# The expert stage of a gated cross-attention block: spreading routing weights over the rows by DMA instead of by a TensorE product, on one Trainium2 core

## The chip, the core and the metric

The kernel runs on one core of one Trainium2 chip. The metric is the device time of one execution in microseconds (us), lower is better. A core has five engines that run side by side, each in its own program order, and that wait for each other through semaphores: PE (TensorE, matrix products into PSUM), DVE (VectorE), ACT (ScalarE), POOL (GpSimd) and SP (SyncE, which here only issues DMAs). SBUF is the working memory of 128 partitions (rows), PSUM the memory that PE writes, in eight banks of 128x512 floats, DRAM the memory of the chip. "PE" in a row of the profile is the matmul itself, "PEld" the load of its stationary operand.

## The reference, cut to what matters

x has 32 batches of 128 tokens with 128 features. The block has four steps, each added to x with a gate: cross attention (stage a), a mixture of eight experts (stage b), a second cross attention with 16 heads (stage c), a second mixture (stage d). The change touches stage b and its two boundaries. Stage b computes:

```python
logits = jnp.einsum('bsd,de->bse', input, Wg)          # input = layernorm(x), E = 8 experts
probs = jax.nn.softmax(logits, axis=-1)
top_vals, top_idx = jax.lax.top_k(probs, TOP_K)        # TOP_K = 2
top_vals = top_vals / jnp.sum(top_vals, axis=-1, keepdims=True)
onehot = jax.nn.one_hot(top_idx, E, dtype=input.dtype)
mask = jnp.sum(onehot, axis=2)
scores = jnp.sum(onehot * top_vals[..., None], axis=2)
xm = input[None] * jnp.moveaxis(mask, -1, 0)[..., None]
h = jnp.einsum('ebsd,edh->ebsh', xm, W1) + b1[:, None, None, :]     # H = 256
h = jax.nn.relu(h)
y = jnp.einsum('ebsh,ehd->ebsd', h, W2) + b2[:, None, None, :]
out = jnp.sum(y * jnp.moveaxis(scores, -1, 0)[..., None], axis=0)
x = x + jnp.tanh(g_ffn[0]) * out
```

All is float32. Products are made from operands that are split in a high and a low part (hi, lo), three PE products each (hi by hi, hi by lo, lo by hi).

## The kernel before

The 32 batches are worked in 8 groups (NG) of 4 batches, 512 tokens (GT) each. In stage b the tokens lie along the columns and the features along the 128 rows. `pipeline` writes each engine's program: `step(a, m, t)` is called with the group m whose experts run, the group a after it, for which things are made ready, and the group t before it, which is finished. Two steps stand in a loop (Fori), the first two and the last are written out. "Group 0" to "group 7" below are the values of m.

Every expert e of a group goes through these steps, all 128 rows high and with two chunks (HC) of 512 columns:

- up (`up`, `hidden_of`): six PE products from xh, xl and W1 into two PSUM banks (L371 to L373); two sets of banks, taken in turn
- relu (L930): ACT adds the bias and writes b_hr, one ACTIVATE for each chunk
- spread (L861): one PE product of a 0/1 matrix with st, which lays row e of the routing weights over all 128 rows, into a PSUM bank; this is the "PE product" of the change
- scale (L978): DVE multiplies b_hr by the spread weights and writes b_hs
- high (L805): ACT rounds b_hs to b_hh; low (L811): DVE writes b_hl = b_hs - b_hh
- down (`down`): six PE products with W2 that add into the bank Y, three experts (LAG) behind up

b_hr, b_hs, b_hh and b_hl have two halves, expert e uses half e % 2. PE runs up e, spread e, down e-3; ACT runs relu e, high e-1; DVE runs scale e, low e-1. Around these, once per group: the weights of the next group are placed in ss (`dve_place`, after expert 0 on DVE), turned by four PE transposes (`place`, expert 2) and copied to st by ACT (`act_place`, expert 3). The finished Y of the group before is copied by ACT ahead of relu 3 (L815), turned back by PE in expert 4 (`y_back`), which also waits for st because both use the bank MISC, added to x by DVE (`dve_residual`) with the statistics of the next layer norm, POOL makes 1/std, DVE norms in expert 5, and xh and xl of the next stage are made in expert 7.

At the front boundary, in the last step of stage a, DVE does the routing of groups 0 to 6 in one piece (`route.first`, `route.second`, then, after xl, `route.weights`); group 7's (`tail`) is done in the first group of stage b, in three pieces at experts 1, 3 and 5. Between them stands the late setup: constants of stage c on DVE (`dve_setup_late`, expert 4), two PE products (L436, L437, expert 5) and an ACT copy (expert 6). At the back boundary, in the last group of stage b and behind it, the first three units of stage c are prepared (`c_prepare`): keys, queries and values of its first group. SP then writes the split keys and queries to DRAM and reads them back spread over partitions, before the first scores (L1177, L1178).

The lines of the profile that the text speaks of, inside the functions that are printed below:

## Time and profile before

| what | us |
|---|---|
| median of 3 runs (their range) | 766.39 (763.78 to 766.4) |
| the profiled execution | 767.7 |
| its span in the trace | 765.9 |
| busy: PE, DVE, ACT, POOL | 649.0, 560.2, 426.0, 104.2 |
| mean granted clock of PE | 0.908 of full speed |
| stage b, from its first relu to the last value of Y (141.85 to 365.9) | 224 |

The profile is of one execution. Busy times of engines overlap, so they don't add up to the span. A row of the timeline is one instruction, or several alike that follow each other (x2 and so on); "[4.67 <-DVE exp_scale L427]" behind it says how long its engine had stood idle and which instruction ended that. A granted clock of 1.00 is 2.4 GHz, of 0.50 is 1.2 GHz.

### The profile page before, as it was taken

How to read it: one execution, taken by the hardware profiler on the slowest of the kernel's cores; microseconds unless marked ns; L12 is line 12 of the kernel's file. 1: busy time of each engine (PE TensorE's matmuls, PEld its weight loads, DVE VectorE, ACT ScalarE, POOL GpSimd, SP SyncE). 2: the span in 40 equal slices, each digit the busy share in tenths (PEclk: the TensorE clock that was granted, in tenths of full speed). 3: DMA queues.
4: the chain of work that ended last, by engine and by line, in shares of the span. 5: the costliest groups of instructions: out<-in, count | busy, mean ns of one | idle time of the engine just before them, and what ended most of it. 6: DMA issues, size and time to landing. Idle time of an engine off the chain costs nothing.

```text
span 765.9 us, 12807 instructions
## 1 busy us (share of the span) xinstructions
PE 649.0 (85%) x4078; PEld 503.5 (66%) x4078; DVE 560.2 (73%) x1281; ACT 426.0 (56%) x665; POOL 104.2 (14%) x133
## 2 busy tenths in 40 slices
PE   5865654979999999979599988988988489999996
PEld 3644443657787787757377666766756267888884
DVE  3567565687898898868478668668676669888885
ACT  3333321467777777756277666656766145555553
POOL 3444230020000000000401022022022100000000
PEclk8677665889999999999799999999999679999998
DMA  5312000000000000010244124224210000000000
GB/s 159 101 63 98 29 8 0 1 0 1 1 0 0 0 0 0 0 43 28 50 121 121 54 67 119 69 49 119 69 42 2 0 1 0 15 14 14 27 14 28
DMA packets 23698, 29.24 MB, mean 38 GB/s; under 512 B 3313, under 2 KB 17522, under 8 KB 23666
## 3 DMA queue, kind: packets, MB, share of 16 engines
q1 hardware_dynamic: 23666, 28.84, 13.1%
...
## 4 chain that ended last, share of the span: by engine, by line
PE 63%; DVE 18%; issue 6%; POOL 5%; ACT 5%; DMA 1%; DVEq 1%; SPq 0%; POOLq 0%; ACTq 0%
PE psum L371 12%; PE psum L373 11%; PE psum L372 11%; PE psum L1187 6%; PE psum L1202 3%; PE psum L1177 2%; DVE stats L281 2%; POOL rstd L293 2%; PE psum L360 2%; PE psum L1178 2%; DVE b_hl L811 2%; DVE xn L300 2%; DVE c_mx L1356 2%; PE psum L1503 2%; PE psum L319 1%
## 5 line engine op out<-in xcount | busy, mean ns | idle before, releaser
L371 PE MATMUL psum<-xh,w_hi 128*128 (+1 forms) x248 | 104.1, 420 | 5.2 <-DVE w_lo L1346 3.0
L1297 ACT ACTIVATE c_pt<-psum 77x512 f32<-77x512 f32 x128 | 74.5, 585 | 49.9 <-PE psum L1187 49.8
L372 PE MATMUL psum<-xl,w_hi 128*128 (+1 forms) x248 | 100.3, 404 | 0.0
L373 PE MATMUL psum<-xh,w_lo 128*128 (+1 forms) x248 | 100.1, 404 | 0.0
L930 ACT ACTIVATE b_hr<-psum,b1s 128x512 f32<-128x512 f32 x128 | 80.8, 686 | 24.0 <-PE psum L373 23.9
L978 DVE TENSOR_TENSOR b_hs<-b_hr,psum 128x1024 f32<-128x1024 f32 x64 | 77.9, 1217 | 21.7 <-ACT b_hr L930 20.4
L811 DVE TENSOR_TENSOR b_hl<-b_hs,b_hh 128x1024 fp32r<-128x1024 f32 x64 | 78.3, 1223 | 16.9 <-ACT b_hh L805 16.9
L805 ACT ACTIVATE b_hh<-b_hs 128x1024 fp32r<-128x1024 f32 x64 | 67.9, 1061 | 34.1 <-PE psum L373 32.2
L1187 PE MATMUL psum<-ident,c_pf 128*77 128x128 f32 x512 | 75.9, 286 | 0.0
L1187 PEld LDWEIGHTS psum<-ident,c_pf 128*77 128x77 f32 x512 | 59.4, 152 | 14.9 <-issue 10.4
L1302 ACT ACTIVATE c_pf<-c_sm,zero_col,exp_scale 128x616 f32<-128x616 f32 x64 | 57.3, 895 | 17.8 <-DVE c_sm L1362 17.8
L1356 DVE TENSOR_REDUCE c_mx<-psum 128x8 f32<-128x616 f32 x64 | 51.0, 797 | 19.8 <-PE psum L1178 19.2
L371 PEld LDWEIGHTS psum<-xh,w_hi 128*128 128x128 f32 x248 | 48.2, 195 | 17.5 <-DVE w_lo L1346 3.4
L1362 DVE TENSOR_TENSOR c_sm<-psum,c_mx 128x616 f32<-128x616 f32 x64 | 51.2, 800 | 6.5
L373 PEld LDWEIGHTS psum<-xh,w_lo 128*128 128x128 f32 x248 | 47.9, 193 | 11.7
L372 PEld LDWEIGHTS psum<-xl,w_hi 128*128 128x128 f32 x248 | 48.2, 194 | 9.5
L805 ACT ACTIVATE d_hh<-d_hs 128x512 fp32r<-128x512 f32 x56 | 35.4, 632 | 31.3 <-DVE d_hs L1598 17.5
L371 PE MATMUL psum<-b_hh,w_hi 128*128 128x512 f32 x128 | 51.5, 403 | 1.4 <-DVE b_hl L811 1.3
L1553 ACT ACTIVATE d_hr<-psum 128x512 f32<-128x512 f32 x56 | 33.4, 597 | 32.7 <-PE psum L373 31.6
...
L1177 PE MATMUL psum<-mask_bf,ident_bf 128*128 128x312 bf16 x128 | 39.1, 312 | 13.9 <-DVE c_sm L1362 10.8
L373 PE MATMUL psum<-b_hh,w_lo 128*128 128x512 f32 x128 | 50.8, 397 | 0.0
...
## 6 DMA issues: line engine op xcount, KB each, us to landing
w_hi<-c_q_spread SPq DMA_DIRECT2D x24, 256.0 KB
...
ctxg<-in_ctxT SPq DMA_DIRECT2D x16, 156.0 KB, 4.1
...
x_all<-in_x SPq DMA_DIRECT2D x8, 256.0 KB, 2.7
out_dram<-x_all SPq DMA_DIRECT2D x8, 256.0 KB, 2.3
...
```

What stands on the lines that cost most here:

```text
L371: pe.matmul(o, wh, h, start=start, stop=False)
L372: pe.matmul(o, wh, l, start=False, stop=False)
L373: return pe.matmul(o, wl, h, start=False, stop=stop)
L805: a_.activation(*self.high(q), ACT.Copy).then_inc(self.hi_done, 1)
L811: v.tensor_tensor(o, i0, i1, ALU.subtract).then_inc(self.lo_done, 1)
L930: ins = a_.activation(Bb["hr"][:, q, c, :], Z[q][c], ACT.Relu, bias=b1s[:, e, c:c + 1])
L978: v.tensor_tensor(Bb["hs"][:, q, :, :], Bb["hr"][:, q, :, :], SBC[q].unsqueeze(1).broadcast_to([P, HC, GT]), ALU.mult).then_inc(xb.scaled, 1)
L1177: pe.matmul(o, ident_bf[:], mask_bf[:].unsqueeze(1).broadcast_to([P, HQ, SK]), start=True, stop=False)
L1187: ins = pe.transpose(bank[2 + q % 2][0:S2, j * P:(j + 1) * P], pf1[:, h % 2, (q % 2) * HQ + j, :], ident[:])
L1297: a_.activation(pt[:, q % NC4, :], bank[2 + q % 2][0:S2, :], ACT.Copy).then_inc(pt_done, 1)
L1302: a_.activation(pf1[:, h % 2, :, :], sm1[:, h % 2, :, :], ACT.Exp, bias=zero_col[:, 0:1], scale=exp_scale[:, 0:1]).then_inc(s1_exp, 1)
L1356: v.tensor_reduce(mm, s, AX.X, ALU.max).then_inc(s1_max, 1)
```

## The change

From group 1 on, row e of the weights comes to the 128 rows by DMA. ss gets a third block, hi + lo (`dve_place`), which the same transposes turn; ACT copies its 8 rows to lt_s; SP stores them to DRAM in two DMAs (b_rows) and reads each row back to all 128 partitions, into one of four slots (SLOTS) of the new tile b_bc. DVE scales with that tile. Group 0 keeps the PE product. To make room, b_hr and b_hs are now the same buffer, and relu waits for `lo_done` where it waited for `scaled`. The routing's second half and the late setup move ahead of stage b (its PE products to bank 5, between the router's product and its transposes); the tail's routing is cut in eight pieces; the prepared units of stage c move from experts 0, 1 (PE) and 1, 2 (ACT, DVE) to 0, 2 and 1, 3; in the last group y_back, residual and norm come one expert later; behind the last group ACT copies xh before it copies the values; SP loads the first context of stage c ahead of its new work.

```diff
@@ pe_setup_late, act_setup_late: bank[7] -> bank[5]
@@ pe_a step
                     lg0.pe_product(pe, t)
+                    if not m:
+                        pe_setup_late(pe)
                     lg0.pe_transpose(pe, t)
@@ act_a step
                     lg0.act_copy(a_, t)
                     if not m:
+                        act_setup_late(a_)
                         Route(0, HEAD, rt_tail).act_ratio(a_)
@@ dve_a step
                         route.first(v)
-                        route.second(v)
...
                     ln1.dve_low(v, t)
                     if not m:
+                        route.second(v)
+                        dve_setup_late(v)
                         route.weights(v)
@@ buffers of stage b
-        B = dict(hr=sb("b_hr", [P, 2, HC, GT]), hs=sb("b_hs", [P, 2, HC, GT]),
+        SLOTS = 4
+        b_hr = sb("b_hr", [P, 2, HC, GT])
+        B = dict(hr=b_hr, hs=b_hr,
                  hh=sb("b_hh", [P, 2, HC, GT], F32R), hl=sb("b_hl", [P, 2, HC, GT], F32R),
-                 y=sb("b_y", [P, 2, GT]))
+                 y=sb("b_y", [P, 2, GT]), bc=sb("b_bc", [P, SLOTS, GT]))
@@ dve_place
-                v.tensor_copy(ss[:, p, :, 32:32 + E], sc_l[:, a.tiles(), :].bitcast(F32)).then_inc(self.ss_ready, 1)
+                v.tensor_copy(ss[:, p, :, 32:32 + E], sc_l[:, a.tiles(), :].bitcast(F32))
+                v.tensor_tensor(ss[:, p, :, 64:64 + E], sc_h[:, a.tiles(), :].bitcast(F32),
+                                sc_l[:, a.tiles(), :].bitcast(F32), ALU.add).then_inc(self.ss_ready, 1)
@@ act_place
+                if self is xb and not self.first(a):
+                    a_.activation(lt_s[64:64 + E, a.parity, :], misc[64:64 + E], ACT.Copy).then_inc(self.rows_done, 1)
                 a_.activation(st[:, a.parity, :], misc, ACT.Copy).then_inc(self.st_done, 1)
@@ new: SP in stage b, ahead of its work for stage c
+        def sp_b(sp):
+            c_prepare["sp"](sp)
+            def step(a, m, t):
+                if not a or xb.first(a):
+                    return
+                p = a.parity
+                sp.wait_ge(xb.rows_done, a.at(1, 0))
+                sp.dma_start(xb.rows_dram[p, 0:4, :], lt_s[64:68, p, :]).then_inc(xb.rows_out[p], 16)
+                xb.before(sp, xb.scaled, a, 0, SLOTS)
+                sp.dma_start(xb.rows_dram[p, 4:E, :], lt_s[68:64 + E, p, :]).then_inc(xb.rows_out[p], 16)
+                for e in range(E):
+                    if e == 0:
+                        sp.wait_ge(xb.rows_out[p], a.pair(32, 32 * p))
+                    else:
+                        xb.before(sp, xb.scaled, a, e, SLOTS)
+                    sp.dma_start(Bb["bc"][:, e % SLOTS, :],
+                                 xb.rows_dram[p, e:e + 1, :].broadcast_to([P, GT])).then_inc(xb.spread_in[e % SLOTS], 16)
@@ pe_b: up, step
-                xb.before(pe, xb.scaled, g, e, 2)
-                pe.matmul(SBC[q], sel0[:, e, :], st[:, g.parity, :], start=True, stop=True).then_inc(xb.bc_ready, 1)
+                if xb.first(g):
+                    xb.before(pe, xb.scaled, g, e, 2)
+                    pe.matmul(SBC[q], sel0[:, e, :], st[:, g.parity, :], start=True, stop=True).then_inc(xb.bc_ready, 1)
...
-                    if m and e == 4 and t:
+                    if m and e == (4 if a else 5) and t:
                         y_back(a, m, t)
...
-                    if m and not a and e < 2:
-                        c_prepare["pe"](pe, e)
+                    if m and not a and e in (0, 2):
+                        c_prepare["pe"](pe, e // 2)
...
-                    if m and e == 5 and xb.first(m):
-                        pe.wait_ge(xb.st_done, 2)
-                        pe_setup_late(pe)
@@ act_b: relu, step
                 xb.before(a_, xb.z_ready, g, e, 0)
-                xb.before(a_, xb.scaled, g, e, 2)
+                xb.before(a_, xb.lo_done, g, e, 2)
...
-                        if xb.first(m) and e == 3:
+                        if xb.first(m) and e == 6:
                             tail.act_ratio(a_)
...
-                        c_prepare["act"](a_, 2)
                         ln2.act_high(a_, t)
+                        c_prepare["act"](a_, 2)
@@ dve_b: scale, step
-                xb.before(v, xb.bc_ready, g, e, 0)
-                xb.before(v, xb.lo_done, g, e, 2)
+                if xb.first(g):
+                    xb.before(v, xb.bc_ready, g, e, 0)
+                    spread = SBC[q]
+                else:
+                    v.wait_ge(xb.spread_in[e % SLOTS], g.at(32, 16 * (e // SLOTS + 1) - 32))
+                    spread = Bb["bc"][:, e % SLOTS, :]
                 v.tensor_tensor(Bb["hs"][:, q, :, :], Bb["hr"][:, q, :, :],
-                                SBC[q].unsqueeze(1).broadcast_to([P, HC, GT]), ALU.mult).then_inc(xb.scaled, 1)
+                                spread.unsqueeze(1).broadcast_to([P, HC, GT]), ALU.mult).then_inc(xb.scaled, 1)
```

Three places in the order of instructions, each in the loop over the middle groups. On ACT, one expert and the start of the next, before:

```order
L930 ACTIVATE b_hr<-psum,b1s 128x512 [waits b_hidden_scaled,b_hidden_ready]
L930 ACTIVATE b_hr<-psum,b1s 128x512
L805 ACTIVATE b_hh<-b_hs 128x1024 [waits b_hidden_used,b_hidden_scaled]
L778 REGISTER_ALU
L930 ACTIVATE b_hr<-psum,b1s 128x512 [waits b_hidden_scaled,b_hidden_ready]
```

and now:

```order
L985 ACTIVATE b_hr<-psum,b1s 128x512 [waits b_hidden_low,b_hidden_ready]
L985 ACTIVATE b_hr<-psum,b1s 128x512
L838 ACTIVATE b_hh<-b_hr 128x1024 [waits b_hidden_used,b_hidden_scaled]
L807 REGISTER_ALU
L985 ACTIVATE b_hr<-psum,b1s 128x512 [waits b_hidden_low,b_hidden_ready]
```

The order is the same; the relu waits for b_hidden_low (counted by low on DVE) in place of b_hidden_scaled (counted by scale). On PE, up of an expert and down of the one three behind it, before:

```order
L371 MATMUL psum<-xh,w_hi 128x512 [waits b_hidden_read]
L372 MATMUL psum<-xl,w_hi 128x512
L373 MATMUL psum<-xh,w_lo 128x512
L371 MATMUL psum<-xh,w_hi 128x512
L372 MATMUL psum<-xl,w_hi 128x512
L373 MATMUL psum<-xh,w_lo 128x512
L861 MATMUL psum<-st,w_hi 128x512 [waits b_hidden_scaled]
L371 MATMUL psum<-b_hh,w_hi 128x512 [waits b_hidden_low]
L372 MATMUL psum<-b_hl,w_hi 128x512
```

and now:

```order
L371 MATMUL psum<-xh,w_hi 128x512 [waits b_hidden_read]
L372 MATMUL psum<-xl,w_hi 128x512
L373 MATMUL psum<-xh,w_lo 128x512
L371 MATMUL psum<-xh,w_hi 128x512
L372 MATMUL psum<-xl,w_hi 128x512
L373 MATMUL psum<-xh,w_lo 128x512
L371 MATMUL psum<-b_hh,w_hi 128x512 [waits b_hidden_low]
L372 MATMUL psum<-b_hl,w_hi 128x512
L373 MATMUL psum<-b_hh,w_lo 128x512
```

The spread product between up and down is gone. On DVE, scale and low of two experts, before:

```order
L978 TENSOR_TENSOR b_hs<-b_hr,psum 128x1024 [waits b_hidden_low,b_spread_ready,b_hidden_read]
L811 TENSOR_TENSOR b_hl<-b_hs,b_hh 128x1024 [waits b_hidden_high,b_hidden_used]
L778 REGISTER_ALU
L978 TENSOR_TENSOR b_hs<-b_hr,psum 128x1024 [waits b_hidden_low,b_spread_ready,b_hidden_read]
L811 TENSOR_TENSOR b_hl<-b_hs,b_hh 128x1024 [waits b_hidden_high,b_hidden_used]
```

and now:

```order
L1049 TENSOR_TENSOR b_hr<-b_hr,b_bc 128x1024 [waits b_spread_loaded2,b_hidden_read]
L844 TENSOR_TENSOR b_hl<-b_hr,b_hh 128x1024 [waits b_hidden_high,b_hidden_used]
L807 REGISTER_ALU
L1049 TENSOR_TENSOR b_hr<-b_hr,b_bc 128x1024 [waits b_spread_loaded3,b_hidden_read]
L844 TENSOR_TENSOR b_hl<-b_hr,b_hh 128x1024 [waits b_hidden_high,b_hidden_used]
```

The order is again the same; scale works in place on b_hr, takes the factor from b_bc and waits for its DMA.

## Rows read from the trace of the kernel before

**Rows 1.** The page, part 4: the chain that ended last, by engine.
```profile
PE 63%; DVE 18%; issue 6%; POOL 5%; ACT 5%; DMA 1%; DVEq 1%; SPq 0%; POOLq 0%; ACTq 0%
```

**Rows 2.** Windows of groups 0, 2, 7: stretch, length, busy by engine, clock, DMA.
```profile
core 0: us, PE busy (x) PEld busy (x) DVE busy (x) ACT busy (x) POOL busy (x), PEclk, DMA share, GB/s
141.85:170.24 28.39, 23.13 (x92) 17.98 (x93) 24.07 (x44) 17.69 (x28) 4.26 (x1) 0.88 0.00 1
...
196.41:222.66 26.25, 26.18 (x119) 21.02 (x118) 22.51 (x35) 19.95 (x27) 1.42 (x3) 1.00 0.00 1
327.70:366.00 38.30, 32.63 (x131) 24.30 (x129) 26.72 (x36) 21.53 (x30) 1.26 (x2) 0.96 0.10 35
```

**Rows 3.** Timeline of PE, group 1: start, duration, engine, line, operation, tiles.
```profile
172.99 0.40 PE L861 MATMUL psum<-st,w_hi 128*128 128x512 f32 x1
...
176.01 0.40 PE L861 MATMUL psum<-st,w_hi 128*128 128x512 f32 x1
```

**Rows 4.** Timeline of ACT, groups 0 and 7.
```profile
154.81 1.26 ACT L930 ACTIVATE b_hr<-psum,b1s 128x512 f32<-128x512 f32 x2
155.95 1.06 ACT L805 ACTIVATE b_hh<-b_hs 128x1024 fp32r<-128x1024 f32 x1
...
339.67 1.26 ACT L930 ACTIVATE b_hr<-psum,b1s 128x512 f32<-128x512 f32 x2 [4.47 <-PE psum L373]
342.26 1.06 ACT L805 ACTIVATE b_hh<-b_hs 128x1024 fp32r<-128x1024 f32 x1 [1.33 <-DVE b_hs L978]
```

**Rows 5.** Timeline of DVE, groups 1 and 7.
```profile
187.87 0.69 DVE L826 TENSOR_TENSOR x_all<-psum,x_all 128x512 f32 x1
...
189.79 1.19 DVE L978 TENSOR_TENSOR b_hs<-b_hr,psum 128x1024 f32<-128x1024 f32 x1
190.90 1.22 DVE L811 TENSOR_TENSOR b_hl<-b_hs,b_hh 128x1024 fp32r<-128x1024 f32 x1
192.03 1.11 DVE L300 TENSOR_SCALAR xn<-x_all,mv,rstd 128x128 f32 x4
...
340.96 1.22 DVE L978 TENSOR_TENSOR b_hs<-b_hr,psum 128x1024 f32<-128x1024 f32 x1 [4.39 <-ACT b_hr L930]
343.42 1.23 DVE L811 TENSOR_TENSOR b_hl<-b_hs,b_hh 128x1024 fp32r<-128x1024 f32 x1 [1.24 <-ACT b_hh L805]
```

**Rows 6.** The page, part 5: busy us, mean ns, idle before, releaser.
```profile
L978 DVE TENSOR_TENSOR b_hs<-b_hr,psum 128x1024 f32<-128x1024 f32 x64 | 77.9, 1217 | 21.7 <-ACT b_hr L930 20.4
L811 DVE TENSOR_TENSOR b_hl<-b_hs,b_hh 128x1024 fp32r<-128x1024 f32 x64 | 78.3, 1223 | 16.9 <-ACT b_hh L805 16.9
```

**Rows 7.** Timeline of PE: the two longest holes of stage b.
```profile
159.68 0.77 PE L436 MATMUL psum<-wo,bv 128*128 128x128 f32 x2 [4.67 <-DVE exp_scale L427]
...
161.09 0.80 PE L371 MATMUL psum<-xh,w_hi 128*128 128x512 f32 x1
...
336.62 0.50 PE L371 MATMUL psum<-xh,w_hi 128*128 128x512 f32 x1 [2.99 <-DVE w_lo L1346]
```

**Rows 8.** Windows behind both holes, and one of stage c.
```profile
159.70:163.80 4.10, 4.10 (x10) 3.09 (x11) 4.10 (x3) 0.00 (x0) 3.03 (x1) 0.50 0.00 0
...
336.60:338.10 1.50, 1.48 (x6) 1.24 (x7) 0.00 (x0) 0.00 (x0) 0.00 (x0) 1.00 0.44 173
338.10:341.30 3.20, 3.20 (x9) 2.47 (x8) 0.34 (x1) 1.26 (x2) 0.00 (x0) 0.50 0.24 72
...
475.00:480.00 5.00, 3.86 (x32) 2.81 (x33) 3.38 (x9) 2.40 (x4) 2.92 (x3) 0.80 0.11 22
```

**Rows 9.** Timeline of DVE at the front boundary: end of second, then xl.
```profile
132.12 0.68 DVE L332 TENSOR_TENSOR xl<-psum,xh 128x512 fp32r<-128x512 f32 x1
```

**Rows 10.** Timeline of ACT and PE at the back boundary.
```profile
374.18 0.68 ACT L1291 ACTIVATE c_v<-psum 77x256 f32<-77x256 f32 x2 [7.64 <-POOL c_v L1440]
...
376.10 0.44 PE L1177 MATMUL psum<-mask_bf,ident_bf 128*128 128x312 bf16 x1 [3.14 <-DVE xl L332]
```

**Rows 11.** DMA issues: tiles, queue, count, KB each, us to landing.
```profile
ctxg<-in_ctxT SPq DMA_DIRECT2D x16, 156.0 KB, 4.1
...
x_all<-in_x SPq DMA_DIRECT2D x8, 256.0 KB, 2.7
```

104 lines of the change are left out of this document (71 added, 33 removed).

## The prediction

> **What bounds the kernel now.** I read the page first: PE holds 63% of the chain that ended last, DVE 18% [rows 1]. Then the windows of the expert stage, cut at the first relu of a group: one of the six groups in the middle takes 26.25 us and PE is busy in 26.18 of them, DVE in 22.51, ACT in 19.95, at a granted clock of 1.00; the first group takes 28.39, the last 38.30 [rows 2]. So in the middle PE is the bound and every matmul removed there would pay its whole pitch, if nothing else comes up. The PE timeline gives that pitch: from one spread product (L861) to the next are 3.02 us and 13 matmuls [rows 3], so 0.23 each. ACT and DVE have what an expert needs of them: relu (two ACTIVATEs), scale (L978), high (L805), low (L811) [rows 4, 5]. Both idle a little per expert, waiting for PE [rows 6].
>
> **Part 1: the spread products.** 56 of the 64 L861 go (groups 1 to 7 have 8 each): 8 x 0.23 = 1.84 us of PE per group. PE then needs 26.25 - 1.84 = 24.4 per group. The scale reads its factor from a 128x512 tile in SBUF, not PSUM. Low has both operands in SBUF and takes 1223 ns where scale with one in PSUM takes 1217 [rows 6], so I take no change for it, and bounds of -0.03 to +0.03 per instruction. The Trainium skill ("VectorE: DVE Perf Modes", the section on the TRN2 errata) has a table with 62 cycles less for an SBUF source than for a PSUM source; by that the scale would be an estimated 0.065 us shorter and this sum some 3.6 us lower. The row of low does not bear that out, and the row decides.
>
> **Part 2: relu now waits for low.** b_hr and b_hs become one buffer, scaled in place. Before, ACT's relu of expert e waited for scale e-2; now for low e-2, since high and low of e-2 still read that half. This is the step that matters. The orders are fixed: ACT runs relu e, high e-1, relu e+1; DVE runs scale e, low e-1, scale e+1. So relu e+1 waits for low e-1, low e-1 stands behind scale e on DVE, and scale e waits for relu e. That is a closed loop, and its length is the time per expert. Its pieces from the traces: relu to scale start 340.96 - 339.67 = 1.29 [rows 4, 5]; scale to low, back to back, 190.90 - 189.79 = 1.11, and low to the next 192.03 - 190.90 = 1.13, I take 1.13; low itself 1.22; from the end of a DVE instruction to the ACT that waited for it 342.26 - (340.96 + 1.22) = 0.08, and I take 0.07 as other rows are a little shorter. Sum 1.29 + 1.13 + 1.22 + 0.07 = 3.71 us. High is beside it: it starts 1.14 after relu and ends at 1.14 + 1.06 = 2.20, and low may start 0.10 later (343.42 after 342.26 + 1.06), at 2.30, before scale lets it at 2.42. So 3.71 against 3.02 now: PE, with 12 x 0.23 = 2.8, waits 0.9 us for each expert. Eight experts: 29.7.
>
> **Part 3: what else sits in the loop.** DVE idles from the pitch of low (1.13) to the next scale (1.22 + 0.07 + 1.29 = 2.58): room for 1.45. Residual and statistics at e = 4 take 189.79 - 187.87 = 1.92 [rows 5], 0.45 too much. Norm, the new third write to ss and the xl of the layer norm fit. On ACT the idle time after high is 1.5: the copy of y, st and the new copy of 8 rows to lt_s, each of 512 columns and so some 0.6 by half a relu (1.27 / 2), fit, the last two together with 0.3 to spare. At e = 4 PE's transposes of y wait for st, which now comes behind that copy, and down 1 behind them reaches high 3 about 0.25 late. Sum 29.7 + 0.45 + 0.25 = 30.4. There is also a hole: PE finds nothing from the end of up 3 until y is copied, by the same addition 3.3 us. The trace has one of 2.99 us in the last group [rows 7]: 1.5 us after it the granted clock fell from 1.00 to 0.50 for 3.2 us [rows 8]. The part of it that isn't absorbed by PE's new slack I put at 0.3 (bounds 0 and 1.6, the second if the clock is low at once, as after the 4.67 us hole [rows 7, 8]). Group: **30.7 us** against 26.25, +4.45, six times: **+26.7**.
>
> **Part 4: first and last group.** In the first, the late setup and the tail's routing held PE up 4.67 us at L436 [rows 7]. The setup goes ahead of the stage and the routing is cut into pieces of under 1.45 us that the loop hides. But the loop holds here too: 8 x 3.71 less 3.71 - 1.14 for the two relus that run back to back = 27.1, against 28.39: **-1.2**, though a hole of 4.67 is gone. The last group has 38.30, with the 2.99 us hole at PE (unit 1 of stage c) and 3.2 at half clock. Afterwards: 7 x 3.71 = 26.0, the 0.7 of part 3, and from the last relu 2.42 + 1.13 + 1.22 and 6 matmuls with their end, 1.6 = 6.4; with 0.3 for the clock 33.4: **-4.9**. The later places of the stage c units are in the idle time of ACT and DVE.
>
> **Part 5: the two boundaries.** Ahead of the stage, second now runs after the xl that waited behind it until 132.12 [rows 9], which frees the router product some 2.6 us earlier; but the late setup now stands ahead of act_ratio and of PE's logit transposes: seven short DVE instructions, an estimated 1.1 in all, two PE products, 161.09 - 159.68 = 1.4 at half clock [rows 7], and an ACT copy, 0.4. Against 2.6 that leaves **+0.3** (bounds -2.6 and +3: all of one side, none of the other). Behind the stage ACT does the xh copy before the value copies, which waited 7.64 for POOL's memset; the scores need those value copies too (374.18 + 0.68 = 374.86), and started at 376.10 [rows 10]: **-1.2**, not more. The key and query DMAs come from an SP queue that now issues them behind the last spread; they still have four experts' time.
>
> **Part 6: the DMAs.** SP gets, per group, two stores of 4x512 and eight spreads of 256 KB, four slots deep. A 256 KB load lands in 2.7 us, a 156 KB one in 4.1 [rows 11]. A slot is asked for when scale e-4 ends, so it has three experts, 11 us. Hidden: 0. The bound above is 4.1 each, one after the other, the rival below. First in a group come the second store, its landing and spread 0, about 2 x 2.7 = 5.4 us of some 11. Hidden too.
>
> **Sum.** 26.7 - 1.2 - 4.9 + 0.3 - 1.2 = **+19.7 us**. Against the profiled span of 765.9 that is 785.6. The profiled execution took 767.7, 1.8 more than its span and 0.2% above the median of the runs, 766.39; so the sum can be laid on the median as it is: **786.1**.
>
> **Rivals.** (a) The clock falls to half at once at each group's restart, or more often: high 2 then waits for a down at half rate, 1.6 us a group, so 32.0: 6 x 5.75 - 1.2 - 3.6 - 0.9 = +28.8, 795.2. For it: a stretch of stage c with gaps of about 1 us and PE busy 3.86 of 5 had 0.80 [rows 8]; against: PE's 25% slack absorbs most. The Trainium skill ("TensorE: Matmul & The Clock Gate", the section on a second HAM failure mode) tells of the same swing where PE idles briefly between groups of matmuls. 0.20. (b) The other side: the loop stays under PE's time, and PE keeps the bound. Then groups take 24.4: 6 x -1.85, the first loses its 4.67 hole, the last 4.9 + 1.85, boundaries -0.9: 11.1 + 4.7 + 6.8 + 0.9 = 23.5 less, 742.9. It decides where the loop is under 24.4 / 8 = 3.05 us; low or scale would have to be half as long, and 64 instances of each say 1.22. 0.05. (c) The spreads come one by one at 4.1 us, 32.8 a group: 39.3 - 1.2 - 2.8 - 0.9 = +34.4, 800.8. Against: 2.7 for a load of this size. 0.04. (d) The in-place wait costs less than read and the stage comes out even, within 0.5%: 0.03.
>
> **Numbers.** Forecast 0.68. A measurement of this kernel can tell about 0.5%, 4 us. Faster by more 0.05, within 0.03, slower 0.92. The range takes in the loop with 0.03 for each handover and no clock loss (30.0 a group, -4.2, and -2.6 of the boundary) and rival (a) with its boundary at +3: 779 to 798.
>
> **What would show it.** Right: group period near 30.7; ACT's b_hr waiting for DVE b_hl, over 0.8 us per expert, as the largest wait of ACT; PE's share of the chain falling and DVE's rising; scale at 1.22. Wrong: b_hr waiting for PE (rival b), scale waiting for a DMA (c), half clock over long stretches (a), or scale much under 1.2.

## The result: 5.6% slower, about twice what was predicted

| | kernel before | changed kernel |
|---|---|---|
| median of the runs (range) | 765.21 (763.5 to 767.48) | 808.03 us (804.57 to 813.07) |
| ratio to before, 95% interval | | 1.056 (1.0523 to 1.0598) |
| span of the profiled execution | 765.9 | 805.6 |
| first relu of stage b | 141.85 | 141.23 |
| group 0 | 28.39 | 28.61 |
| groups 1 to 6, mean | 26.24 | 33.33 |
| group 7, to the copy of Y | 38.27 | 37.39 |
| Y to the end of the span | 399.96 | 398.38 |

A group runs from its first relu to that of the next, read from the timeline of ACT. The prediction was 786.1 us, range 779 to 798: the sign is right, the time lies 22 us above it and outside the range. The excess of 39.7 us in the span lies in groups 1 to 6 alone: 6 x (33.33 - 26.24) = 42.5, where the prediction had 26.7. The rest of the program came out 2.8 us shorter.

The page of the changed kernel, part 4 (answers to [rows 1]) and three groups of part 5 (busy us, mean ns, idle before, releaser; answer to [rows 6]):

```profile
PE 45%; DVE 24%; issue 10%; ACT 10%; POOL 8%; DVEq 1%; DMA 0%; ACTq 0%; SPq 0%; POOLq 0%
...
L985 ACT ACTIVATE b_hr<-psum,b1s 128x512 f32<-128x512 f32 x128 | 80.9, 684 | 87.9 <-DVE b_hl L844 81.0
...
L1049 DVE TENSOR_TENSOR b_hr<-b_hr,b_bc 128x1024 f32<-128x1024 f32 x56 | 68.3, 1220 | 52.3 <-ACT b_hr L985 52.3
...
L844 DVE TENSOR_TENSOR b_hl<-b_hr,b_hh 128x1024 fp32r<-128x1024 f32 x64 | 78.0, 1219 | 12.3 <-ACT b_hh L838 12.3
```

PE's share of the chain fell from 63 to 45%. The relu (L985) idles 81.0 us behind low (L844), scale (L1049) 52.3 us behind relu, and never behind a DMA. One turn of the loop, from the timelines of ACT and DVE in group 2:

```profile
207.31 1.27 ACT L985 ACTIVATE b_hr<-psum,b1s 128x512 f32<-128x512 f32 x2 [1.63 <-DVE b_hl L844]
208.61 1.23 DVE L1049 TENSOR_TENSOR b_hr<-b_hr,b_bc 128x1024 f32<-128x1024 f32 x1 [1.12 <-ACT b_hr L985]
209.75 1.22 DVE L844 TENSOR_TENSOR b_hl<-b_hr,b_hh 128x1024 fp32r<-128x1024 f32 x1
211.06 1.26 ACT L985 ACTIVATE b_hr<-psum,b1s 128x512 f32<-128x512 f32 x2 [1.54 <-DVE b_hl L844]
```

1.30 + 1.14 + 1.22 + 0.09 = 3.75 us, as summed (3.71). The windows, cut as in [rows 2], give group 2 and the last:

```profile
203.47:237.08 33.61, 27.39 (x110) 20.12 (x110) 22.63 (x36) 20.08 (x28) 3.29 (x3) 0.95 0.20 63
...
369.83:407.22 37.39, 31.87 (x117) 23.90 (x117) 25.18 (x34) 21.00 (x29) 2.97 (x2) 0.86 0.22 71
```

Group 2 from relu to relu: 3.84 + 3.75 + 3.75 + 5.27 + 4.50 + 4.17 + 4.63 + 3.70 = 33.61. Eight plain experts would be 30.0, so 3.6 us lie in four intervals. **Experts 3 to 5**, timelines of PE and ACT:

```profile
213.81 0.75 PE L927 MATMUL psum<-st,w_hi 128*128 128x512 f32 x1 [3.04 <-ACT b_y L848]
214.36 0.63 PE L928 MATMUL psum<-st,w_lo 128*128 128x512 f32 x1
...
217.59 1.06 ACT L838 ACTIVATE b_hh<-b_hr 128x1024 fp32r<-128x1024 f32 x1 [1.52 <-PE psum L373]
...
222.10 1.06 ACT L838 ACTIVATE b_hh<-b_hr 128x1024 fp32r<-128x1024 f32 x1 [0.75 <-PE psum L373]
```

PE stands 3.04 us for the copy of y (predicted: 3.3). Then its matmuls of 512 columns take 0.63 instead of 0.39, at half the clock, 1.2 of 2.4 GHz (granted 0.51 in the window 213.80 to 217.00, below). High 2 waits 1.52 for down 0. High 3 waits 0.75 for down 1, which stands behind the transposes of y, and these wait 1.04 for st. **Experts 5 and 6**, timelines of DVE and POOL:

```profile
226.33 1.20 DVE L1049 TENSOR_TENSOR b_hr<-b_hr,b_bc 128x1024 f32<-128x1024 f32 x1
226.49 1.08 POOL L257 TENSOR_TENSOR spare_q<-half_neg 1x1 f32<-1x1 f32 x1 [30.29 <-DVE mv L284]
227.44 1.22 DVE L844 TENSOR_TENSOR b_hl<-b_hr,b_hh 128x1024 fp32r<-128x1024 f32 x1
227.55 1.20 POOL L292 TENSOR_SCALAR vpe<-mv 128x4 f32<-128x4 f32 x1
228.83 1.04 POOL L293 TENSOR_TENSOR rstd<-vpe,half_neg 128x4 f32<-128x4 f32 x1
229.90 1.12 DVE L300 TENSOR_SCALAR xn<-x_all,mv,rstd 128x128 f32 x4 [1.24 <-POOL rstd L293]
```

POOL's first operation for 1/std ends as scale does (227.57 and 227.53), its second as low does (228.75 and 228.66). Before, they took 0.18 and 0.22:

```profile
189.96 0.18 POOL L257 TENSOR_TENSOR spare_q<-half_neg 1x1 f32<-1x1 f32 x1 [24.93 <-DVE mv L284]
190.12 0.22 POOL L292 TENSOR_SCALAR vpe<-mv 128x4 f32<-128x4 f32 x1
190.42 1.04 POOL L293 TENSOR_TENSOR rstd<-vpe,half_neg 128x4 f32<-128x4 f32 x1
```

### The profile page after: what moved, and what is told of

Its sections match the earlier page's. It is cut to its first block, busy times and chain, and to the rows that moved or that the text cites. A ratio compares the mean times of both kernels' runs of the same rounds, so it can differ in the third digit from the quotient of the medians.

```text
span 805.6 us, 12850 instructions
## 1 busy us (share of the span) xinstructions
PE 654.0 (81%) x4022; PEld 495.9 (62%) x4022; DVE 558.5 (69%) x1297; ACT 427.4 (53%) x672; POOL 117.3 (15%) x133
## 4 chain that ended last, share of the span: by engine, by line
PE 45%; DVE 24%; issue 10%; ACT 10%; POOL 8%; DVEq 1%; DMA 0%; ACTq 0%; SPq 0%; POOLq 0%
PE psum L371 7%; PE psum L373 7%; PE psum L372 7%; PE psum L1261 5%; DVE b_hl L844 5%; ACT b_hr L985 3%; POOL rstd L293 3%; DVE b_hr L1049 3%; PE psum L1276 3%; DVE xn L300 3%; DVE stats L281 3%; PE psum L1251 2%; ACT b_hh L838 2%; PE psum L360 2%; PE psum L1252 2%
## 5 line engine op out<-in xcount | busy, mean ns | idle before, releaser
L985 ACT ACTIVATE b_hr<-psum,b1s 128x512 f32<-128x512 f32 x128 | 80.9, 684 | 87.9 <-DVE b_hl L844 81.0
L1049 DVE TENSOR_TENSOR b_hr<-b_hr,b_bc 128x1024 f32<-128x1024 f32 x56 | 68.3, 1220 | 52.3 <-ACT b_hr L985 52.3
L844 DVE TENSOR_TENSOR b_hl<-b_hr,b_hh 128x1024 fp32r<-128x1024 f32 x64 | 78.0, 1219 | 12.3 <-ACT b_hh L838 12.3
L838 ACT ACTIVATE b_hh<-b_hr 128x1024 fp32r<-128x1024 f32 x64 | 67.7, 1058 | 14.1 <-PE psum L373 11.3
L371 PE MATMUL psum<-b_hh,w_hi 128*128 128x512 f32 x128 | 57.4, 448 | 12.7 <-DVE b_hl L844 12.7
L257 POOL TENSOR_TENSOR spare_q<-half_neg 1x1 f32<-1x1 f32 x24 | 9.8, 410 | 369.9 <-DVE mv L284 369.9
L319 PE MATMUL psum<-ident,xn 128*128 128x128 f32 x128 | 26.1, 338 | 40.4 <-DVE xn L300 27.7
L372 PE MATMUL psum<-b_hl,w_hi 128*128 128x512 f32 x128 | 53.8, 420 | 0.0
L373 PE MATMUL psum<-b_hh,w_lo 128*128 128x512 f32 x128 | 53.4, 418 | 0.0
```

What stands on the lines that cost most here:

```text
L371: pe.matmul(o, wh, h, start=start, stop=False)
L372: pe.matmul(o, wh, l, start=False, stop=False)
L373: return pe.matmul(o, wl, h, start=False, stop=stop)
L838: a_.activation(*self.high(q), ACT.Copy).then_inc(self.hi_done, 1)
L844: v.tensor_tensor(o, i0, i1, ALU.subtract).then_inc(self.lo_done, 1)
L985: ins = a_.activation(Bb["hr"][:, q, c, :], Z[q][c], ACT.Relu, bias=b1s[:, e, c:c + 1])
```

## The experiments

Each was timed beside the kernel before, and its ratio is to those runs, whose medians were 766.4 to 767.2 us. "1 to 6" is the mean of groups 1 to 6, "tail" the stretch from the last relu of stage b to the copy of Y, all read from the timeline of ACT.

| kernel | median us | ratio (95% interval) | group 0 | 1 to 6 | last | tail |
|---|---|---|---|---|---|---|
| before (profiled) | 765.21 | 1 | 28.39 | 26.24 | 38.27 | 8.43 |
| changed | 808.03 | 1.056 (1.0523, 1.0598) | 28.61 | 33.33 | 37.39 | 9.92 |
| e4_in_place_alone | 806.41 | 1.0514 (1.0481, 1.0547) | 33.11 | 31.50 | 40.18 | 7.15 |
| e5_placement_alone | 758.61 | 0.9878 (0.9834, 0.9923) | 20.84 | 26.24 | 33.91 | 9.54 |
| e1_two_buffers | 763.14 | 0.9955 (0.9931, 0.9979) | 20.83 | 26.97 | 36.28 | 12.43 |
| e2_early_y | 809.58 | 1.0554 (1.0514, 1.0593) | 28.64 | 33.49 | 37.97 | 9.90 |
| e3_psum_factor | 799.34 | 1.0427 (1.0395, 1.046) | 28.64 | 31.76 | 36.11 | 8.68 |
| e9_expert5_psum | 801.64 | 1.0465 (1.0414, 1.0516) | 28.62 | 31.78 | 37.36 | 9.90 |
| e8_no_hole | 806.73 | 1.0511 (1.0463, 1.0559) | 29.27 | 32.74 | 38.11 | 9.93 |
| e11_hole_and_pool | 796.55 | 1.0407 (1.034, 1.0474) | 28.30 | 31.35 | 36.61 | 9.92 |
| e14_last_transposes | 809.97 | 1.0594 (1.0549, 1.0639) | 28.63 | 33.04 | 41.11 | 13.61 |
| e15_last_expert6 | 809.17 | 1.0543 (1.0495, 1.0591) | 28.61 | 33.24 | 35.60 | 8.90 |
| e17_last_norm | 806.89 | 1.0544 (1.0508, 1.0581) | 28.62 | 33.03 | 38.66 | 8.36 |
| e10_all | 764.21 | 0.9971 (0.9943, 0.9999) | 22.23 | 26.68 | 34.87 | 10.81 |
| e13_best | 759.34 | 0.9902 (0.987, 0.9933) | 20.84 | 25.78 | 39.98 | 16.09 |
| **e16_two_buffers_psum5_6** | **752.19** | 0.9801 (0.9775, 0.9828) | 20.83 | 25.77 | 35.20 | 11.05 |
| e18_two_buffers_norm | 751.19 | 0.9823 (0.9782, 0.9863) | 20.83 | 25.78 | 34.58 | 8.67 |

### The wait for low: the loop

e4_in_place_alone, on the kernel before (b_pad keeps the addresses of the rest; the last two lines are relu's wait; "..." in a diff stands for lines left out):

```diff
-        B = dict(hr=sb("b_hr", [P, 2, HC, GT]), hs=sb("b_hs", [P, 2, HC, GT]),
+        b_hr, pad = sb("b_hr", [P, 2, HC, GT]), sb("b_pad", [P, 2, HC, GT])
+        B = dict(hr=b_hr, hs=b_hr,
...
-                xb.before(a_, xb.scaled, g, e, 2)
+                xb.before(a_, xb.lo_done, g, e, 2)
```

> The kernel before with one part of the change alone: b_hr scaled in place and relu waiting for low e-2. Spread products on PE, no DMAs, boundary work where it was. Theory of the loop: 3.75 us per expert, 31 to 33 us a group against 26.25, and the holes of the first and last group come on top: 800 to 812 us. Rival, that the DMA path is what costs: 764 to 772.

e1_two_buffers, on the changed kernel (to make room, the spread has 2 slots and b_y one half; a transfer of 16 bytes carries one wait on SP; the last lines are relu's wait and scale's):

```diff
-        B = dict(hr=b_hr, hs=b_hr,
+        B = dict(hr=b_hr, hs=sb("b_hs", [P, 2, HC, GT]),
...
-                xb.before(a_, xb.lo_done, g, e, 2)
+                xb.before(a_, xb.scaled, g, e, 2)
...
+                xb.before(v, xb.lo_done, g, e, 2)
```

> The changed kernel with b_hr and b_hs apart again: relu waits for scale e-2, scale for low e-2, as before the change. To make the room, the spread tile has two slots in place of four and b_y one half; the two stores of the rows go out together. Theory of the loop (relu, scale, low e-1, relu): the loop is cut, PE's 24.4 us or the spreads set the group, 24.4 to 26.3 us a group, 750 to 768 us in all. Rival, that the DMA spreads or the moved boundary work cost the time: groups stay over 30 us and the time over 790.

With the wait alone, the kernel before goes to 806.41; without it, the changed kernel to 763.14. A stretch of eight experts of each, from the windows; that of e4 runs from relu 3 of group 2 to relu 3 of group 3, that of e1 is its group 2:

```profile
218.53:248.98 30.45, 27.00 (x119) 20.78 (x119) 22.38 (x34) 19.33 (x27) 1.42 (x3) 1.00 0.00 0
```

```profile
192.80:219.76 26.96, 25.22 (x111) 19.30 (x111) 22.51 (x36) 20.57 (x29) 3.29 (x3) 1.00 0.28 80
```

The first, of e4, has no transfer in it and all spread products, and takes 30.45 us, close to the 30.4 of the prediction's sum without its clock term. In part that is luck: the 0.25 for high 3 is not in it (e4 has no copy of 8 rows), and the 0.04 by which a turn is longer than summed, eight times, fills its place. The wait alone costs nearly as much as the whole change, and the transfers are not what costs. It doesn't cost it in the same places: in groups 1 to 6 e4 loses 6 x (31.50 - 26.24) = 31.6 us of the 42.5 of the changed kernel, and 6.6 more in its first and last group, where the work of the boundaries still has its old places. The second, of e1 with two slots, shows it once more: 80 GB/s run beside a group of 26.96.

### The placement alone

e5_placement_alone: the spread products of all groups and both buffers are back, stores and spread transfers are gone, the new places of the boundary work stay. The lines are in PE's spread and in relu's wait.

```diff
-                if xb.first(g):
+                if True:
...
-                xb.before(a_, xb.lo_done, g, e, 2)
+                xb.before(a_, xb.scaled, g, e, 2)
```

> Edit, on the changed kernel: the spread products of TensorE for all groups, relu and scale in separate buffers as before, neither the stores of the eight rows nor the transfers that spread them; what stays is the placement of the boundary work anew (setup ahead of the stage, the tail's routing cut in pieces, the earlier pieces of the next stage, three blocks of ss). Theory (the placement is no part of the slowdown and gives back some of the holes of the first and the last group and of the boundary behind the stage): groups 1 to 6 at 26.2 us as before, 3 to 6 us gained outside them: 760 to 764 us. Rival (the placement costs part of the slowdown, by new holes or by work in other queues): 768 us or more.

It is 1.2% faster than the kernel before, with groups of 26.24 us as there. Its first group takes 20.84, where [rows 2] has 28.39 and a clock of 0.88: the hole of 4.67 us in [rows 7] is gone and with it the half clock.

```profile
145.00:165.84 20.84, 20.26 (x88) 15.99 (x89) 19.06 (x32) 17.69 (x27) 4.28 (x1) 1.00 0.00 0
```

The gain is more than the 3 to 6 us expected. In the changed kernel the loop takes it back: 28.61, and e1, without the loop, has 20.83.

### POOL held up by DVE

e3_psum_factor: in groups 1 to 7, too, scale reads a factor from PSUM, a stale one of group 0; their weighting by their own weights is left out.

```diff
-                    spread = Bb["bc"][:, e % SLOTS, :]
+                    spread = SBC[q]
```

> The changed kernel, but DVE's scale takes its factor from the PSUM bank that group 0 left, in all groups; the DMAs and their waits stay. It leaves out that groups 1 to 7 are scaled with their own weights. Theory that POOL stands still while DVE works on two SBUF operands: POOL's two short instructions ahead of 1/std take 0.2 each again and not 1.1 and 1.2, norm no longer waits, relu 5 to 6 and 6 to 7 go to 3.75 each; 1.3 us less per group and some 2 to 3 at the end of the last, 796 to 800 us. Rival, that POOL is late because of the DMAs or of low: POOL as in the changed kernel, within 2 us of 808.

e9_expert5_psum keeps the spread product for expert 5 alone:

```diff
-                if xb.first(g):
+                if xb.first(g) or e == 5:
...
+                    if e == 5:
+                        v.wait_ge(xb.bc_ready, g.at(1, 8))
+                        spread = SBC[q]
```

> Edit, on the changed kernel: for expert 5 of every group TensorE's spread product stays and the scale of expert 5 takes its second operand from PSUM; the transfer of that row and all other experts stay as they are. It is the scale that ran beside GpSimd's subtraction for the standard deviation. Theory (a VectorE operation with both operands in SBUF holds up GpSimd's two tiny operations for the normalisation, 1.08 and 1.20 us instead of 0.18 and 0.22, and VectorE then waits 1.24 us for their result): the subtraction goes back to about 0.2 us; the second one, beside the product low of expert 5 which has both operands in SBUF in the kernel before too, where it was not held up, also; relu 5 to relu 7 falls from 8.8 us to about 7.5, a group by 1.3, seven groups by 9: time 798 to 801 us. Rival (the late standard deviation comes from somewhere else, or only moves the wait): 806 to 809 us.

Both give POOL its short times back, here e9, DVE and POOL:

```profile
224.75 1.19 DVE L1052 TENSOR_TENSOR b_hr<-b_hr,psum 128x1024 f32<-128x1024 f32 x1
224.92 0.18 POOL L257 TENSOR_TENSOR spare_q<-half_neg 1x1 f32<-1x1 f32 x1 [29.72 <-DVE mv L284]
225.08 0.22 POOL L292 TENSOR_SCALAR vpe<-mv 128x4 f32<-128x4 f32 x1
225.38 1.04 POOL L293 TENSOR_TENSOR rstd<-vpe,half_neg 128x4 f32<-128x4 f32 x1
225.86 1.22 DVE L844 TENSOR_TENSOR b_hl<-b_hr,b_hh 128x1024 fp32r<-128x1024 f32 x1
227.00 1.11 DVE L300 TENSOR_SCALAR xn<-x_all,mv,rstd 128x128 f32 x4
```

POOL starts 0.17 us behind scale here and 0.16 in the changed kernel, so that it is the operand that differs and not the moment. Relu 6 to relu 7 falls from 4.62 to 3.76, 0.87 a group, not the 1.3 expected: relu 5 to relu 6 stays at 4.17, which is residual and statistics. The mean group falls by 1.55; the rest is the clock, which in e9 fell in only three of these six groups. The Trainium skill ("SBUF — State Buffer", the section "SBUF: two separate sides") says that a DVE instruction with two SBUF inputs and a POOL instruction that reads SBUF exclude each other, and that the second waits for the whole of the first; for POOL behind DVE the rows agree, to 0.1 us. For DVE behind POOL they don't: above, low with its two SBUF inputs starts 0.48 us into POOL's 1/std, and neither takes longer.

### The hole and the clock

e2_early_y copies Y one expert earlier:

```diff
-                        if e == LAG and t:
+                        if e == LAG - 1 and t:
                             xb.act_y(a_, t, Y)
```

> The changed kernel with ACT's copy of y ahead of relu 2 in place of relu 3. Theory of the clock: the 3.0 us hole of PE in front of b2 goes, the clock stays at 1.00 behind it, down 0 takes 1.4 and not 2.5, and relu 3 to relu 4 falls from 5.27 to about 3.9; 1.3 to 1.6 us less per group, 797 to 800 us in all against 808. Rival, that the low clock lies in slack and relu 4 is late by something else: within 2 us of 808.

The hole only moved, behind st, and the half clock with it (PE of e2):

```profile
218.70 1.11 PE L853 MATMUL psum<-ident,b_y 128*128 128x128 f32 x4 [4.23 <-ACT st L832]
...
220.04 0.63 PE L372 MATMUL psum<-b_hl,w_hi 128*128 128x512 f32 x1
```

e8_no_hole adds to this the placement one expert earlier on PE and ACT:

```diff
-                    if m and e == 2 and a:
+                    if m and e == 1 and a:
                         place(a)
...
-                        if e == 3 and a:
+                        if e == 2 and a:
                             xb.act_place(a_, a, MISC)
```

> Edit, on the changed kernel: the copy of the Y bank stands before expert 2 on ScalarE instead of before expert 3, the placement before expert 1 on TensorE instead of before expert 2, and ScalarE's copies of its result before expert 2 instead of before expert 3, so that neither the b2 matmul nor the transposes of y find their operand late. In the changed kernel relu 3 to relu 4 took 5.27 us and relu 4 to relu 5 4.50 where a plain expert takes 3.75. Moving the copy of Y alone left the sum of two experts at 9.75 us, with a new hole of 4.23 us at the transposes. Theory (TensorE's holes of 3 to 4 us at the boundary bring the granted clock to half, and the work behind them runs at half): without the hole the two intervals come to about 8.3 us together instead of 9.77, a group to about 31.9 instead of 33.3 us, and seven groups with a boundary give 8 to 10 us: a span of about 796 us, time 797 to 800. Rival (the boundary costs what it does through ScalarE's and VectorE's queues, whatever TensorE's clock): 805 to 809 us, as the changed kernel.

e11_hole_and_pool is e8 and e9 together.

> Edit, on the changed kernel: both edits together, the boundary's copies and the placement moved as in the one and expert 5's factor from PSUM as in the other. Theory (the two are independent, and with both gone a group is what the prediction summed without a clock term: eight times 3.71 plus 0.7 = 30.4 us): group about 30.5 us, seven intervals of groups 20 us shorter than in the changed kernel: time 787 to 791 us. Rival (they share one cause, or each only hides the other): no less than the better of the two alone, 797 us or more.

e8 reached 806.73, not 797 to 800: a hole of some 2.4 us came up at the placement, behind ss. In groups 2 and 3 of e8 (PE, then windows):

```profile
208.31 0.66 PE L825 MATMUL psum<-ident,ss 128*128 128x128 f32 x4 [2.47 <-DVE ss L819]
...
241.76 0.66 PE L825 MATMUL psum<-ident,ss 128*128 128x128 f32 x4 [2.43 <-DVE ss L819]
```

```profile
204.23:237.66 33.43, 27.58 (x110) 20.01 (x110) 22.45 (x36) 19.86 (x28) 3.28 (x3) 0.95 0.21 64
237.66:269.61 31.95, 25.87 (x111) 18.97 (x111) 22.58 (x36) 19.87 (x28) 3.28 (x3) 1.00 0.20 66
```

Two like holes, one with the clock down behind it and one without; the difference, 1.5 us, is what this fall costs. The same in the changed kernel and e9, both with a hole of 3.04 us that ends at 213.81, 213.80 to 217.00 of each:

```profile
213.80:217.00 3.20, 3.19 (x8) 2.51 (x9) 1.81 (x2) 1.26 (x2) 0.00 (x0) 0.51 0.28 87
```

```profile
213.80:217.00 3.20, 3.19 (x14) 2.55 (x14) 1.81 (x2) 2.19 (x3) 0.00 (x0) 1.00 0.30 87
```

8 matmuls in one, 14 in the other. Groups 2 and 5 of e9 are 31.16 and 32.70. So the length of a hole alone doesn't say whether the clock falls. In the changed kernel it fell in all six groups (mean 0.95 in each), and what that cost depends on when: relu 3 to relu 4 took 4.88 to 5.27 us in five of them and 4.15 in group 4, where the half clock came 1.5 us behind the hole and met only the last two of down 0's six products:

```profile
280.72 0.50 PE L927 MATMUL psum<-st,w_hi 128*128 128x512 f32 x1 [3.04 <-ACT b_y L848]
...
281.98 0.47 PE L371 MATMUL psum<-b_hh,w_hi 128*128 128x512 f32 x1
282.24 0.63 PE L372 MATMUL psum<-b_hl,w_hi 128*128 128x512 f32 x1
```

A fall thus cost 0.4 to 1.5 us there, 1.2 in the mean. The Trainium skill ("TensorE: Matmul & The Clock Gate", the section "What's actually happening") calls the gate's activity window free-running. By that, the moment at which a hole comes would count besides its length; that fits these pairs, but no run shows it. e11 gives the sum of both edits: five of its six groups took 31.01 to 31.29 us (clock 1.00 in groups 2 and 3), one 32.64. That is some 0.7 above the 30.4 without clock term: 0.45 more in the interval at the placement (4.20 instead of 3.75), 0.3 in the turn of the loop, 0.2 in two intervals of 3.85, less the 0.25 of high 3, which waits no longer. Its time, 796.55, lies 6 us above the range expected; for six groups these 0.7 and the one fall are 5.7 of them.

### The last group

e14_last_transposes puts PE's transposes of the norm of group 6 behind two down products:

```diff
-                    if m and e == 7 and t:
+                    if a and e == 7 and t:
                         ln2.pe_transpose(pe, t)
+                    if t and not m and e == 1:
+                        ln2.pe_transpose(pe, Group(None, NG - 2))
```

> Edit, on the changed kernel: in the last group only, TensorE's transposes for the normalisation of the group before stand behind the second product of experts 5 and 6 instead of ahead of them. In the changed kernel TensorE waited there 4.55 us for the normalised rows and then ran nine matmuls and more at half the clock, and from relu 7 to the copy of Y it took 9.9 us, where the prediction had 6.4. Theory (the transposes in a queue that runs in order hold up two products whose operands are there, and the hole halves the clock behind them): the hole shrinks to about 1.5 us or less in one piece, relu 7 to the copy of Y takes 7 to 7.6 us: the span shorter by 2.3 to 2.9 us, time about 805 us. Rival (the tail is set by VectorE's chain of norm, scale 7, xl and low 7 alone): 9.5 to 9.9 us, no gain.

e15_last_expert6, in the last group alone:

```diff
-                if xb.first(g):
+                if xb.first(g) or (g.i is None and g.c == NG - 1 and e == 6):
...
+                    if g.i is None and g.c == NG - 1 and e == 6:
+                        v.wait_ge(xb.bc_ready, 9)
+                        spread = SBC[q]
```

> Edit, on the changed kernel: in the last group only, the spread product of expert 6 stays on TensorE and its scale reads the factor from PSUM; that scale ran beside GpSimd's two operations for the standard deviation, and in the last group, unlike the others, TensorE's transposes wait for the rows that follow from it. Theory (part of the last group's 3.5 us too much is GpSimd held up again, 1.11 and 1.86 us there): GpSimd is done before VectorE asks for it, the normalisation starts 0.93 us earlier, TensorE's hole falls from 4.55 to 3.6 us; a hole of that length still halves the clock, so that relu 7 to the copy of Y takes 8.9 to 9.1 us instead of 9.9. Rival (the shorter hole leaves the clock alone, as the 3.1 us hole of the group with an undisturbed clock would have it): 6.9 to 7.3 us.

PE's transposes in the changed kernel, the first down of e14 and ACT's xh there, the transposes of e15:

```profile
399.31 1.11 PE L319 MATMUL psum<-ident,xn 128*128 128x128 f32 x4 [4.55 <-DVE xn L300]
```

```profile
396.14 0.50 PE L371 MATMUL psum<-b_hh,w_hi 128*128 128x512 f32 x1 [2.51 <-DVE b_hl L844]
...
403.90 0.60 ACT L326 ACTIVATE xh<-psum 128x512 fp32r<-128x512 f32 x1 [5.51 <-PE psum L319]
```

```profile
400.44 1.12 PE L319 MATMUL psum<-ident,xn 128*128 128x128 f32 x4 [3.44 <-DVE xn L300]
...
402.21 0.63 PE L373 MATMUL psum<-b_hh,w_lo 128*128 128x512 f32 x1
```

e14 refuted its theory. The down products weren't held up by the transposes alone: the first of them waited 2.51 us for its own operand. Then xh came late, high 7 behind it in ACT's order, and the tail grew to 13.61 us. In e15 the tail took 8.90, as its theory had it: 1.0 us is POOL, and the clock is still halved behind the hole of 3.44.

e4, with the work of the last group placed as before, has no hole at these transposes and a tail of 7.15:

```profile
395.56 0.60 PE L319 MATMUL psum<-ident,xn 128*128 128x128 f32 x4
...
401.15 0.50 PE L371 MATMUL psum<-b_hh,w_hi 128*128 128x512 f32 x1 [2.09 <-DVE b_hl L812]
401.49 0.39 PE L372 MATMUL psum<-b_hl,w_hi 128*128 128x512 f32 x1
```

The change had moved the residual and the norm of the last group one expert later, and e17_last_norm undoes that (in order: transposes of y, residual, norm):

```diff
-                    if m and e == (4 if a else 5) and t:
+                    if m and e == 4 and t:
...
-                        if e == (4 if a else 5) and t:
+                        if e == 4 and t:
...
-                        if e == (5 if a else 6) and t:
+                        if e == 5 and t:
```

> Edit, on the changed kernel: in the last group the transposes of y, the residual with its statistics, and the norm stand at experts 4, 4 and 5 again, as in all other groups and as in the kernel before, not at 5, 5 and 6. With the in-place wait alone, where they stood so, PE's transposes in expert 7 found the normalised rows ready, the clock stayed at 1.00 and the stretch from the last relu to the copy of Y was 7.15 us; in the changed kernel they wait 4.55 us and the stretch is 9.92. Theory (the tail's excess is this later place, which leaves one expert less between norm and transposes, and the half clock behind the hole that comes of it): the hole goes, the stretch is 7.1 to 7.6 us; PE may wait 1 to 2 us more in expert 4, where its transposes of y need the second unit of stage c to have been read: last group 35 to 36.5 us instead of 37.4; time 806 to 807. Rival (the hole comes from GpSimd's lateness and the operands in SBUF): stretch of 9 us or more.

```profile
384.79 0.66 PE L853 MATMUL psum<-ident,b_y 128*128 128x128 f32 x4 [1.85 <-DVE w_lo L1420]
...
396.60 0.60 PE L319 MATMUL psum<-ident,xn 128*128 128x128 f32 x4
...
402.36 0.51 PE L371 MATMUL psum<-b_hh,w_hi 128*128 128x512 f32 x1 [2.08 <-DVE b_hl L844]
```

The transposes of the norm now follow without a wait, and the tail is 8.36: the later norm and its hole made the most of it. 7.1 to 7.6 were expected; the last down product ran at half clock here, behind two holes of 1.40 and 2.08. In e4 it ran at full clock behind two of 1.24 and 2.09, and that is the difference to 7.15. But y's transposes now wait 1.85 us for the second unit of stage c, with the half clock behind them, and the last group as a whole takes 38.66, more than before the edit.

### A version that beats both

e10_all is two buffers with the edits of e8 and e9. e13_best is two buffers with those of e9 and e14. e16_two_buffers_psum5_6 is two buffers with that of e9, and that of e15 in the last group; e18_two_buffers_norm is two buffers with those of e9 and e17.

> Edit: both of those, and the products of relu and scale in two buffers, so that relu e waits for scale e-2 only (763.1 us with the buffers alone, group 26.9 us). Theory (the wait in place, the hole and GpSimd's lateness are all that stands between this form and one bound by TensorE's matmuls without the spread products): plain experts about 2.8 us, boundary experts 3.2 to 3.6 instead of 3.65 to 4.6, a group of 24.6 to 25.5 us, time 745 to 755 us, below the kernel before by 1.5 to 3 in a hundred. Rival (VectorE, at 2.8 us for a plain expert plus the boundary's work of about 3 us, is the bound now): group 25.8 to 26.5 us, 757 to 762 us.

> Edit, on the kernel with two buffers (763.1 us, groups of 26.9): the spread product and its PSUM operand kept for expert 5, and the last group's transposes behind the products of experts 5 and 6. The copies and the placement at the boundary stay where the changed kernel has them, since with two buffers their earlier place cost 3.6 us in a row (relu 1 to relu 2 took 6.4 instead of 2.8 us, since ScalarE stood before the copy of Y while the relu behind it was ready). Theory (GpSimd's late result is the largest thing left in a group, 4.59 instead of 2.8 us in one expert, and then TensorE is what bounds the plain experts): groups of 25.3 to 25.7 us, the last group 2 us shorter: 752 to 756 us, 1.5 to 2 in a hundred below the kernel before. Rival (something else is next at once, the copies at the boundary or VectorE): groups of 26.3 to 26.9, 758 to 763 us.

> Edit, on the kernel with two buffers: the spread product and PSUM operand kept for expert 5 of every group and, in the last group, for expert 6; the transposes of the last group stand where the changed kernel has them, since moving them cost time (relu 7 to the copy of Y 13.6 us instead of 9.9 in the changed kernel, 16.1 instead of 12.5 with two buffers). Theory: groups of 25.75 us as measured without the change in the last group, and in the last group a hole of TensorE of about 1.7 us instead of 3.17, short enough for the full clock, as in the kernel with the placement alone, where relu 7 to the copy of Y took 9.5 us: together 6 to 7 us less than with the moved transposes: 752 to 755 us, below the placement alone (758.6). Rival (the clock falls in the last group all the same): 755 to 757 us.

> Edit, on the kernel with two buffers: the factor of expert 5 from PSUM in every group, and the residual and norm of the last group at experts 4 and 5, so that expert 5's PSUM operand covers them there too. The version with expert 6's factor from PSUM in the last group instead had 752.2 us, groups of 25.77, a last group of 35.2 and from the last relu to the copy of Y 11.05 us, with a hole of 1.91 us and the half clock behind it. Theory: same groups, PE's transposes without a hole, from the last relu to the copy of Y 8.5 to 9.5 us, last group 33.0 to 34.0: 750 to 751.5 us. Rival (PE's wait in expert 4 for the second unit of stage c takes the gain back): 752 to 754.

e10 was expected at 745 to 755 us and took 764.21. With the faster experts the early copy of Y blocks ACT, since Y isn't finished, and relu 2 stands behind it (ACT of e10; relu 1 to relu 2 takes 6.40 to 6.72 us in groups 1 to 6):

```profile
200.43 0.60 ACT L851 ACTIVATE b_y<-psum 128x512 f32<-128x512 f32 x1 [3.42 <-PE psum L373]
```

e13 has the short groups (25.78) and loses 3.7 us of them in the tail, 16.09 against 12.43 of e1, by the edit that e14 refuted. e16 leaves it out: 752.19 us, 2.0% under the kernel before (interval 1.7 to 2.3%). A group of it, and the transposes of its last group:

```profile
189.31:215.11 25.80, 24.74 (x113) 19.67 (x112) 22.52 (x36) 20.69 (x28) 1.42 (x3) 1.00 0.27 84
```

```profile
345.36 0.99 PE L319 MATMUL psum<-ident,xn 128*128 128x128 f32 x4 [1.91 <-DVE xn L300]
...
346.57 0.63 PE L372 MATMUL psum<-b_hl,w_hi 128*128 128x512 f32 x1
```

PE is busy in 24.74 of 25.80 us and nearly the bound again. Two buffers thus fit beside the spread tile, with two slots for it and one half of b_y; the room didn't force the shared buffer. e18 takes this hole away, too, has a tail of 8.67 and 751.19 us, the same within the intervals; its last group got 0.6 shorter, half of what was expected or less. Both beat the kernel before and the changed one. Against e5 the groups 1 to 6 are 0.47 us shorter, which is all that fewer products on PE were worth once the loop and POOL were out of the way, and the last group is 1.3 us longer in e16: 1.5 us in stage b. The spans differ by 6.6 (759.6 and 753.0). The rest lies ahead of and behind stage b, where both do the same work, and I have no cause for it; the four runs of e5 lie from 754.2 to 762.1 us, so a part of it can be scatter.

## Why the prediction was off, point by point

The mechanism was right: the closed loop of relu, scale and low sets the group, and it was summed to 0.04 us a turn. The steps that failed are terms beside the loop. Part 3 put nothing for POOL at the norm, 0.3 for the clock and 0.25 for high 3, and the runs show 0.87, 1.2 and 0.7 a group. Part 4 summed the last group's tail to 6.4 us, and it took 9.9. In the spans 20 us are missing from the forecast: 15.8 in groups 1 to 6 (6 x 2.63), 4.0 in the last group and 1.4 in the first, less 1.3 at the two boundaries.

- **What bounds the kernel; part 2, the loop.** Right: 3.75 us a turn against 3.71, relu waiting for low the largest wait of ACT, scale at 1220 ns. Eight times 0.04 are 0.3 of the 2.6 us by which the forecast group was too short.
- **Part 1.** Right: scale with an SBUF operand takes 1220 ns against 1217, not the estimated 65 ns less by the table of the Trainium skill ("VectorE: DVE Perf Modes", the section "The TRN2 errata"). The form of the operand did cost, but by way of POOL.
- **Part 3, "norm ... fit".** This step failed. DVE's time was counted, not when POOL would deliver: 0.87 us a group (4.63 instead of 3.75, e9), at DVE's norm. The prediction has no word on POOL's part in the norm. [rows 5] would have been no warning: there low, with two SBUF operands, takes its usual 1.22 us beside POOL, which had started first.
- **Part 3, the clock.** The mechanism and the hole (3.04 against 3.3) were right, the size was not: 0.3 was put in where a fall costs up to 1.5 (e8). Groups of e9 at full clock took 31.2; with POOL's 0.87 that leaves 33.33 - 32.1 = 1.2 for the mean group. PE's slack absorbs little of it, since high 2, inside the loop, waits for the product at half rate. Rival (a) had about this price (1.6); its 795.2 lacked POOL, the later high 3, the longer turn and the tail of the last group.
- **Part 3, the rest.** Residual and statistics 0.42 against 0.45: right. High 3 behind down 1: 0.7 (4.44 instead of 3.75 in groups of e9 at full clock) against 0.25. The excesses are 0.3 (turn) + 0.45 (high 3) + 0.9 (clock) + 0.87 (POOL) = 2.5 of the 2.63 by which 33.33 exceeds 30.7.
- **Part 4, first group.** Forecast -1.2 (27.1 less 28.39 is -1.3), measured +0.2. The intervals behind the first two relus were 4.45 and 4.12 instead of 3.71, the first since the place of ss and a piece of the routing stand between scale 0 and scale 1; for the second no run shows a cause.
- **Part 4, last group.** Forecast -4.9, measured -0.9. The failed term is the tail: 6.4 summed, 9.9 measured. The sum had no term for the later norm of this group, nor for PE's transposes that stand behind it, in front of three down products: the hole of 4.55 and the half clock. POOL makes 1.0 of it (e15), the later place 1.6 (e17; the two may overlap). Even in e4, without that hole, the tail is 7.15.
- **Part 5.** Front -0.6 against +0.3, back (Y to the first scores) 9.06 against 10.16 = -1.1 against -1.2: right, though the first relu lay between 141.2 and 145.0 in the kernels of this study, so the front can't be told from nothing.
- **Part 6.** Right: the spreads land in 3.1 us, and no scale waits for one.
- **Rivals (b) to (d)** fell. The range ended where rival (a) did, without room for a cost that I hadn't named.

What stays open: what besides a hole's length makes the clock fall, and the 3 us that are left of the slowdown when the wait (e4, +39.5 us against its runs of before), the placement (e5, -7.8) and POOL with the clock falls that went with it (from e9, +7.9) are taken from +42.8.
